# A three-stage block (graph convolution, selective scan, top-2 experts): the experts' norm factor taken from the first variance, and its input moved ahead of the router's chain

## The reference, cut to what matters

```python
t = t + _L1_ffn_ref(_ln_t(t), ...)           # _ln_t: (v - m) / sqrt(s + 1e-5), over the 64 channels
# inside _L1_ffn_ref
logits = xt @ Wr + br                          # router, from the once-normed tokens
probs = softmax(logits); top_p, top_idx = top_k(probs, 2)
weights = top_p / top_p.sum()
var = ((xt - mu) ** 2).mean(); xn = (xt - mu) * rsqrt(var + 1e-5)   # a second norm of the same tokens
h = gelu((xn * ln_g + ln_b) @ W1 + b1); y = h @ W2 + b2
out = sum of weights * y over the 2 chosen experts
```

## Time and profile before

| what | us |
|---|---|
| median of 3 runs (lowest, highest) | 497.2 (494.56, 501.62) |
| the profiled execution, its time | 496.86 |
| the profiled execution, its span | 495.1 |
| PE busy (matmul) | 383.4 (77%) |
| DVE busy | 361.2 (73%) |
| ACT busy | 282.0 (57%) |
| POOL busy | 236.6 (48%) |
| start of DVE's gate (L674) in bodies 1 to 7 and the tail | 116.13, 177.42, 223.90, 270.39, 316.87, 363.34, 410.76, 456.75 |

### The profile page before, as it was taken

The page is one execution under the profiler, slowest core; times in us unless marked ns, Lnnn a source line. Parts: engine busy times, 40 slices in busy tenths (PEclk is TensorE's granted clock), DMA queues, the critical chain, the costliest instruction groups (busy, mean ns, idle before and its releaser), DMA issues.

```text
span 495.1 us, 5681 instructions
## 1 busy us (share of the span) xinstructions
PE 383.4 (77%) x1815; PEld 216.9 (44%) x1815; DVE 361.2 (73%) x532; ACT 282.0 (57%) x457; POOL 236.6 (48%) x215
## 2 busy tenths in 40 slices
PE   0867860276669888987998899879968977895895
PEld 0653630023534355544543554455535534452653
DVE  3756329857945889789979997998879787876412
ACT  1022653445464868586858785786758563851463
POOL 5342004664134581766376457727682674375013
PEclk9989765567877999999999999999989998999899
DMA  9560299999989997798799869996997787000000
GB/s 206 147 108 1 59 224 222 220 216 215 219 198 226 194 228 170 171 222 204 155 212 213 212 150 216 212 220 140 216 224 171 169 201 151 1 1 1 11 0 11
DMA packets 23829, 78.40 MB, mean 158 GB/s; under 512 B 5213, under 2 KB 13561, under 8 KB 15609
## 3 DMA queue, kind: packets, MB, share of 16 engines
q1 hardware_dynamic: 22920, 77.74, 70.1%
q10 hardware_dynamic: 880, 0.32, 0.3%
HBM read 72.81 MB, written 5.24 MB: 158 GB/s over the span
## 4 chain that ended last, share of the span: by engine, by line
PE 37%; DMA 15%; DVE 15%; ACT 10%; issue 8%; POOL 8%; SPq 5%; DVEq 0%; POOLq 0%
PE P L1055 11%; DMA ub<-u_scratch 7%; PE P L1041 7%; POOL hs L325 7%; DMA av<-dt_scratch 6%; PE P L1042 5%; DVE hs L646 4%; ACT av L482 3%; PE P L951 3%; PE P L1028 2%; PE P L1071 2%; DVE P L639 2%; ACT L578 2%; DMA hb<-in_L_ffn_W 1%; PE P L995 1%
## 5 line engine op out<-in xcount | busy, mean ns | idle before, releaser
L325 POOL TENSOR_TENSOR hs<-hs,Cs 128x1024 f32<-128x1024 f32 x64 | 151.6, 2371 | 133.2 <-DVE hs L646 133.2
L646 DVE TENSOR_TENSOR_SCAN hs<-av,P 128x1024 f32<-128x1024 f32 x64 | 146.3, 2286 | 6.5 <-POOL av L318 4.5
L527 ACT ACTIVATE hb<-P,b1c 128x512 f32<-128x512 f32 x128 | 81.3, 685 | 38.6 <-PE P L1042 37.1
L1071 PE MATMUL P<-W1H,WzH 128*128 128x512 f32 x338 | 100.6, 435 | 0.0
L482 ACT ACTIVATE av<-av,Aneg 128x510 f32<-128x510 f32 x128 | 83.4, 707 | 28.7 <-DMA av<-dt_scratch 28.6
L639 DVE SCALAR_TENSOR_TENSOR P<-P,bbcol,ub 128x1024 f32<-128x1024 f32 x64 | 82.3, 1286 | 18.1 <-DMA ub<-u_scratch 17.5
L1071 PEld LDWEIGHTS P<-W1H,WzH 128*128 128x128 f32 x338 | 64.3, 197 | 21.8 <-issue 9.3
L1055 PE MATMUL P<-hb,W2s 128*64 128x256 f32 x512 | 71.7, 403 | 0.0
L1041 PE MATMUL P<-X,W1H 128*128 128x512 f32 x128 | 59.7, 466 | 9.2 <-ACT hb L527 7.5
L759 DVE SCALAR_TENSOR_TENSOR mes<-P,cols,wbs 128x256 f32<-128x256 f32 x64 | 27.8, 476 | 51.0 <-PE P L1055 51.0
L951 PE MATMUL P<-hs,selS 128*32 128x512 f32 x256 | 35.6, 650 | 32.5 <-POOL hs L325 32.5
(11 more groups left out here) (182 smaller groups left out, 447.0 us busy)
## 6 DMA issues: line engine op xcount, KB each, us to landing
av<-dt_scratch SPq DMA_DIRECT2D x32, 1024.0 KB, 7.2
ub<-u_scratch SPq DMA_DIRECT2D x32, 1024.0 KB, 11.4
dt_scratch<-dts SPq DMA_DIRECT2D x8, 256.0 KB, 4.2
u_scratch<-rl SPq DMA_DIRECT2D x8, 256.0 KB, 3.5
av<-in_L_conv_Wr SPq DMA_DIRECT2D x2, 576.0 KB, 7.0
av<-in_L_conv_Wl SPq DMA_DIRECT2D x2, 576.0 KB, 8.7
res<-in_x SPq DMA_DIRECT2D x4, 256.0 KB, 4.9
hb<-in_L_ffn_W SPq DMA_DIRECT2D x2, 512.0 KB, 6.2
```

The lines of the kernel that those rows point to most:

```text
L325: gp.tensor_tensor(hs[:, at, :, :], hs[:, at, :, :], rep(Cs[:, p, :], 1, 2), ALU.mult).then_inc(S["cm"], 1)
L527: a_.activation(hb[:, r % 4, :], P[:, (XA, XB)[r % 2], :], ACT.Gelu, bias=b1c[:, r:r + 1]).then_inc(S["gl"], 1)
L646: v.tensor_tensor_scan(hs[:, (SLOTS * g + n) % RING].rearrange("p a t -> p (a t)"), av[:, 2 * n:2 * n + 2, :].rearrange("p a t -> p (a t)" ...
L1071: pe.matmul(P[:, bank, :], WzH[:, :], W1H[:, 0:2, :].rearrange("p e f -> p (e f)"), start=True, stop=True)
```

## The change

It does five things. The second factor is computed from the first variance by a Ln with scale 1+e and bias e² and an Exp, without `r2s` and `vqs`. Both Ln's now stand ahead of both Exp's in `act_lnF2`. `dve_xn2` reads the centred token in PSUM instead of `tns` in SBUF. The router's logits go to bank XA instead of XB, so `pe_router` waits for `tn` and for the relu that reads XA (`sp_relu`), and the first expert product waits for `lgb`, the reader of the logits. And DVE does `dve_xn2` ahead of `dve_router1` and `dve_router2`, in the bodies and in the tail. The orders of PE and of ACT are otherwise what they were.

```diff
@@ constants
             gp.memset(epst[:, :], EPS).then_inc(S["k_misc"], 1)
+            gp.memset(eps2t[:, :], EPS * EPS).then_inc(S["k_misc"], 1)
             gp.memset(onet[:, :], 1.0).then_inc(S["k_misc"], 1)
@@ ACT
         def act_lnF2(eng, g):
             eng.wait_ge(S["var2"], g + 1)
             since(eng, "tn", g)
-            since(eng, "r2", g)
             a_.activation(rs2[:, :], P[:, XB, HW:T], ACT.Ln, bias=epst[:, 0:1]).then_inc(S["ln2"], 1)
+            since(eng, "xn2", 2 * g)
+            a_.activation(rqs[:, :], P[:, XB, HW:T], ACT.Ln, scale=1.0 + EPS, bias=eps2t[:, 0:1]).then_inc(S["lnq"], 1)
             eng.wait_ge(S["ln2"], g + 1)
             a_.activation(rs2[:, :], rs2[:, :], ACT.Exp, scale=-0.5).then_inc(S["rs2"], 1)
-            eng.wait_ge(S["rs2"], g + 1)
-            since(eng, "vq", g)
-            a_.activation(r2s[:, :], rs2[:, :], ACT.Square).then_inc(S["r2"], 1)
-
-        def act_lnF3(eng, g):
-            eng.wait_ge(S["vq"], g + 1)
-            since(eng, "xn2", 2 * g)
-            a_.activation(rqs[:, :], vqs[:, :], ACT.Ln, bias=epst[:, 0:1]).then_inc(S["lnq"], 1)
             eng.wait_ge(S["lnq"], g + 1)
             a_.activation(rqs[:, :], rqs[:, :], ACT.Exp, scale=-0.5).then_inc(S["rq"], 1)
...
-            eng.wait_ge(S["k_misc"], 3)
+            eng.wait_ge(S["k_misc"], 4)
...
                 if prev is not None:
-                    act_lnF3(eng, prev)
                     act_router(eng, prev)
@@ DVE
         def dve_lnF(eng, g):
             eng.wait_ge(S["rs2"], g + 1)
-            since(eng, "lg", g)
-            since(eng, "xn2", 2 * g)
+            since(eng, "lg", 2 * g)
             v.tensor_tensor(tns[:, :], P[:, XB, 0:HW], rs2[:, :], ALU.mult).then_inc(S["tn"], 1)
-
-            eng.wait_ge(S["r2"], g + 1)
-            since(eng, "lnq", g)
-            v.tensor_tensor(vqs[:, :], P[:, XB, HW:T], r2s[:, :], ALU.mult).then_inc(S["vq"], 1)
 
         def dve_xn2(eng, g):
             eng.wait_ge(S["rq"], g + 1)
-            eng.wait_ge(S["tn"], g + 1)
             since(eng, "xl2", g)
...
-                v.tensor_tensor(xnt2[:, HW * h:HW * h + HW], tns[q, :], rqs[q, :], ALU.mult).then_inc(S["xn2"], 1)
+                v.tensor_tensor(xnt2[:, HW * h:HW * h + HW], P[q, XB, 0:HW], rqs[q, :], ALU.mult).then_inc(S["xn2"], 1)
@@ DVE, router1
-            v.tensor_tensor(rt[:, 0], P[:, XB, 0:4 * EXP].rearrange("p (c e) -> p c e", e=EXP),
+            v.tensor_tensor(rt[:, 0], P[:, XA, 0:4 * EXP].rearrange("p (c e) -> p c e", e=EXP),
@@ DVE, body
                 if prev is not None:
+                    dve_xn2(eng, prev)
                     dve_router1(eng, prev)
                     dve_router2(eng, prev)
-                    dve_xn2(eng, prev)
@@ DVE, tail
             dve_lnF(eng, G - 1)
+            dve_xn2(eng, G - 1)
             dve_router1(eng, G - 1)
-            dve_xn2(eng, G - 1)
             dve_router2(eng, G - 1)
@@ PE
         def pe_router(eng, g):
             eng.wait_ge(S["tn"], g + 1)
-            eng.wait_ge(S["vq"], g + 1)
+            eng.wait_ge(S["sp_relu"], so_far(g, 2))
             for q in range(2):
-                pe.matmul(P[:, XB, 2 * EXP * q:2 * EXP * q + 2 * EXP], tns[:, 128 * q:128 * q + 128],
+                pe.matmul(P[:, XA, 2 * EXP * q:2 * EXP * q + 2 * EXP], tns[:, 128 * q:128 * q + 128],
@@ PE, f1
             if r == 0:
                 eng.wait_ge(S["xl2"], g + 1)
-                eng.wait_ge(S["sp_relu"], so_far(g, 2))
-            if r == 1:
                 eng.wait_ge(S["lgb"], g + 1)
```

More of the change, by code:

```diff
@@ L57 @@
 bm scan cm ysum
-yg po t1 cen2 sq2 var2 ln2 rs2 r2 vq lnq rq tn xn2 xh2 xl2
+yg po t1 cen2 sq2 var2 ln2 rs2 lnq rq tn xn2 xh2 xl2
 lg lgb m1 dd ex s1 ms1 o1 e2 m2 s2 s2r ms2 o2 den rden num wt vhi vlo wtr wtc wb_mm wb
@@ L118, in build @@
         epst = sb("epst", [128, 1])
+        eps2t = sb("eps2t", [128, 1])
         onet = sb("onet", [128, 1])
@@ L165, in build @@
         rs2 = sb("rs2s", [128, HW])
-        r2s = sb("r2s", [128, HW])
-        vqs = sb("vqs", [128, HW])
         rqs = sb("rqs", [128, HW])
@@ L617, in _ @@
             act_lnF2(eng, G - 1)
-            act_lnF3(eng, G - 1)
             act_router(eng, G - 1)
@@ L1154, in _ @@
             outputs(3)
-            eng.wait_ge(S["k_misc"], 13)
+            eng.wait_ge(S["k_misc"], 14)
             eng.wait_ge(S["res_ready"], 1)
```

## The result

The changed kernel takes 503.13 us (median of 4 runs, 499.08 to 504.84), the kernel before 497.51 us (494.56 to 501.62). The ratio on record is 1.0185, 95% interval [1.0134, 1.0235], about 9.2 us slower, where 9.6 were forecast. It is not the ratio of the two medians, which are 5.6 us apart (1.0113); which runs of the kernel before it is taken over is not known. So the loss is known as 6 to 9 us. The profiled execution of the changed kernel is its fastest: 499.08 us, span 497.3, only 2.2 us over the profiled one of before. So the two traces hold something that hides most of the loss.

The account below looks back on a forecast made before the run. The bound was taken to be the chain of waits from router through transposes to first Gelu. Terms 7.2 + 2.0 - 0.7 + 0.0 by order plus 1.1 for the clock, on 496.86, gave 506.5 us, range 503 to 510.

Parts of the forecast that it names:

- The sum: Whole kernel: 8.5 us by order and 1.1 for the clock, 9.6 us added to 496.86.
- The chain: Bodies, norm to first Gelu: each microsecond by which the router ends later moves the first Gelu and the body by one.
- The term of 1.8 us: Bodies 2 to 5, router start on DVE: +0.23 - 0.45 + 2.08, taken as 1.8 us later each, 7.2 in all.
- Nothing in the chain gets shorter: Router's first operation to the transposes: no step shortens, so the transposes move from 235.29 to 237.1.
- The source in PSUM: dve_xn2 on DVE: reading PSUM instead of SBUF costs zero, as both pairs of products took 0.87 us.
- Bodies 6 and 7: Router on DVE: part of the 2.08 us fills its wait for matmuls; +1.0 us each, 2.0 for both.
- The tail: After the last body: the router starts earlier and the transposes come at 470.7 instead of 471.42, -0.7 us.
- The clock: PE ahead of the transposes, bodies 2 to 5: a longer gap can drop the clock, 0.5 us a drop, 1.1 taken.
- Body 1: Weights come 1.8 us later, still over 3 us before the awaited transfer lands: zero if the clock behaves as before.
- rival A: Body 1, PE ahead of pair 1: shorter gap keeps the clock high, 6 us less, 500.5 us; chance 0.25.
- B: Bodies: something other than the weights releases the first Gelu, hiding the later router; 494.9 us; chance 0.05.
- C: Bodies 2 to 5: clock drops in every longer gap and stays low through pair 1, 2 us each; 513.4 us; chance 0.1.

Follow-up runs that it names:

- e6: Changed kernel with idle PE products filling the gap ahead of the transposes, plus 16 behind body 1's first spread of the weights: 498.6 us, ratio to before 1.0105.
- e4: Kernel before with 16 idle PE products behind the first spread of the weights in body 1: 492.62 us, ratio 0.9957.
- e2: Kernel before with only dve_xn2 moved ahead of dve_router1 and dve_router2 in the bodies: 513.28 us, ratio 1.0355.
- e10: Kernel before, unchanged, run for a second profile: 494.49 us (one execution).
- e11: Changed kernel, unchanged, run for a second profile: 505.06 us (one execution).
- e1: Changed kernel with dve_xn2 put back behind dve_router1 and dve_router2 in the bodies, all else kept: 491.72 us, ratio 0.997.
- e5: e1 with POOL's product of slot 1 held back until DVE has split the inputs of the experts and the next group: 492.27 us, ratio 0.9971.

## Why the prediction was right

*The number.* The time of 503.13 us is 3.4 below the forecast of 506.5 and inside the range. The sum began at a profiled execution of 496.86 us, and the kernel before has medians of 494.3 to 494.9 in the later measurements; that accounts for 2.0 to 2.6 us. The two second profiles differ by 10.6 us, the ratio on record says 9.2, e6 against e4 6.0 to 7.3, and the sum was 9.6.

*The chain.* Right. The transposes released ACT, and the loss up to the transposes (1.63 us in body 3) came out at the next gate as 1.65.

*The term of 1.8 us.* Its parts: the second Ln 0.22 (0.23 forecast), the start of the router against the gate 8.93 us instead of 7.10, +1.83 (1.8). But the transposes moved by 1.63 only, because the router's chain became 0.20 us shorter: the subtraction, 0.39 us before, is 0.19 after. Ahead of the change it stood in POOL's product, too, which the prediction did not see. "Nothing in the chain gets shorter" is the sentence that failed, by a tenth of the term. These are the rows of DVE and of POOL in body 3 of the kernel before:

```profile
231.45 0.39 DVE L713 TENSOR_TENSOR rt<-rt,rv 128x32 f32<-128x32 f32 x1
```

```profile
229.41 2.37 POOL L325 TENSOR_TENSOR hs<-hs,Cs 128x1024 f32<-128x1024 f32 x1 [0.33 <-DVE hs L646]
```

The idle time of ACT ahead of the router's Exp was forecast 1.8 us longer and is 2.44 longer (0.69 to 3.13).

*The source in PSUM:* cost zero, right, and for less than the whole reason. The 0.87 us from SBUF had been read where POOL's product was over. At the new place the products run beside it, and from SBUF they took 0.44 us more in e2, with 0.58 us of POOL's product left at their start. In the changed kernel 1.03 us of it are left, so by estimate the source in PSUM spares it that much or more.

*Bodies 6 and 7:* 1.0 each was forecast. The start of the router against `tns` moved by 0.75 and 1.22 (2.40 and 2.87, from 1.65). In body 6 the rest of the 1.46 is `tns` itself, 0.69 later against the gate in these two profiles. In body 7 the cast of the experts' input took 0.87 us instead of 0.42; it ended at 420.76, and POOL's product at 420.49. Another 0.54 of body 7's 1.80 lies behind the first Gelu (29.50 us to the next gate, 28.96 before); e10 has 29.48 there, so that part is the execution's. These two rows are of DVE and of POOL in body 7 of the changed kernel:

```profile
419.89 0.87 DVE L685 CAST X<-xnt 64x512 fp32r<-64x512 f32 x1
```

```profile
418.12 2.37 POOL L324 TENSOR_TENSOR hs<-hs,Cs 128x1024 f32<-128x1024 f32 x1 [3.04 <-DVE hs L637]
```

*The tail:* -0.7 forecast. From the Ln to the transposes it was 8.40 us and is 7.68: -0.72. The other 0.6 of the profile's -1.34 lies ahead of the Ln, which comes 5.63 us behind the gate instead of 6.27, and is an earlier return of the clock: the averaging product just ahead of it takes 0.59 us instead of 0.85.

*The clock:* 1.1 us for bodies 2 to 5 was forecast, at 0.5 for a drop. The profiles show 1.0 (two drops) and 3.0 (four). The price of one is right (0.36 to 0.53) but for one of 1.66. The forecast took a little above two drops; two profiles don't tell the mean number. A drop in body 7 of e11 was not in the sum at all.

*Body 1.* Zero was forecast for the likeliest case and 6 us for rival A. The first profile took A in full, the second took none of it against before's second (58.01 and 58.24). So body 1 varies by the execution in both kernels, 61.3 and 58.2 before, 55.2 and 58.0 after, and which of them a profile catches is luck. The length of the gap ahead of pair 1, on which A was built, does not settle it: e1 has a gap of 2.50 us and keeps the clock behind it (29.94 us from the first Gelu to the next gate), e11 has 2.30 and loses it for a while (33.04). Whether the change makes a low clock in body 1 rarer is not shown.

*Rivals B and C* are out: B by bodies of 48.1 us, C by drops of 0.5 us where 2 was its price. One drop of six, in body 3 of e11, came near that price with 1.66 us.

## What to carry to other kernels

A value made early helps only if the engines that use it also reach their use early: before one step of a hand-written list is moved, look at what the next engines have queued ahead of it. Here the same change costs up to 1.9% by itself and stands in a kernel that is 3.7% faster once the lists of ACT and PE follow; how much of that gain needs the new order is open. And where one profile of a kernel that idles PE differs from the next by 6 us, compare body by body and stretch by stretch, not end to end.

## What was unexpected of the hardware

A short DVE operation can be held until a POOL product ends. In every case seen the held operation reads two tensors in SBUF, or is a cast from SBUF to SBUF. A held operation on 32 elements of two tensors ends 0.04 to 0.06 us behind POOL's `hs` product, a held cast 0.27 to 0.29 us behind it, or in the prologue behind another POOL product. Examples are the subtraction in body 3 of the kernel before (0.39 us instead of 0.19, end 231.84, POOL's end 231.78), that in e1 (0.63, 224.65 and 224.60), and the cast in body 7 above. Operations with one operand in PSUM run beside the same product at their usual length, as `tns` and `xnt` at 223.80 and 224.14 do with POOL busy from 223.69. In body 1 a DVE operation of 0.19 us takes 2.15 for the same reason, beside a POOL product of 2.36 (timelines of DVE and of POOL, the changed kernel):

```profile
127.12 2.15 DVE L708 TENSOR_TENSOR rt<-rt,rv 128x32 f32<-128x32 f32 x1
```

```profile
126.86 2.36 POOL L324 TENSOR_TENSOR hs<-hs,Cs 128x1024 f32<-128x1024 f32 x1
```

The Trainium skill, page "SBUF — State Buffer", section "SBUF: two separate sides", states this as an exclusive lock: whichever of the two starts first keeps the shared pair of ports for its whole instruction, and a DVE operation needs it with two SBUF inputs or in a two-port mode. e5 agrees: with POOL's product moved away the subtraction is back at 0.19 us. It is why taking `vqs` off DVE gains nothing while the router stands first: the router then only reaches the held step sooner (transposes 11.40 us behind the gate in e1, 10.96 in e5, where nothing holds it).
